# Six PSUM banks in one pool in place of two rings of three, in a kernel of two FFNs around a state-space layer

## What is computed

```python
def ffn(x):                                    # I = 2048 hidden
    h = silu(x @ w_gate) * (x @ w_up)
    return sparsify_2to4(h) @ w_down
def mamba(x):                                  # E = 1024, N = 16, after an RMS norm
    skip, u = xn @ W_skip.T, silu(causal_conv4(xn @ W_in.T) + conv_b)
    delta = softplus(u @ Wd1.T @ Wd2.T + bd2)
    h[l] = exp(delta[l] * A) * h[l-1] + delta[l] * u[l] * B[l]     # scan over 512 tokens, per (e, n)
    y = (sum_n h * C + u * W_D) * silu(skip)
    return y @ W_out.T
x = x + 0.5 * ffn(layernorm(x)); x = x + mamba(layernorm(x)); x = x + 0.5 * ffn(layernorm(x))
```

## Time and profile before

| | us |
|---|---|
| runs | 3585.91, 3588.35, 3592.87 |
| median | 3588.35 |
| profiled execution | 3583.97 |
| its span | 3582.0 |
| mean granted TensorE clock | 0.98 |

### The profile page before, as it was taken

One profiled execution on the slowest core, in us unless ns is written; L12 is line 12 of the kernel. 1 busy time (PEld: TensorE's weight loads), 2 busy tenths in 40 slices (PEclk: granted clock), 3 DMA queues, 4 the chain that ended last, 5 costly groups with the idle time before them and its releaser, 6 DMA issues. The chain is left out here.

```text
span 3582.0 us, 38967 instructions
## 1 busy us (share of the span) xinstructions
PE 3358.4 (94%) x11958; PEld 2126.1 (59%) x12020; DVE 3028.8 (85%) x3597; ACT 2001.7 (56%) x2760; POOL 2598.5 (73%) x1625
## 2 busy tenths in 40 slices
PE   8999999999999999999999999998979889988899
PEld 6775667556655665556655665555545555555567
DVE  5546998789999889989898899988998988999934
ACT  5546657557565665566555675555555566454422
POOL 1315876667877779868787789878888878989913
PEclk9999999999999999999999999999999989999999
DMA  9656566657656666466665675646646556545433
GB/s 361 218 188 194 171 211 214 212 177 223 211 182 215 199 222 211 158 211 214 185 210 179 203 229 177 217 147 210 222 125 211 169 179 220 189 146 190 138 124 115
DMA packets 243469, 696.44 MB, mean 194 GB/s; under 512 B 23536, under 2 KB 23792, under 8 KB 233584
## 3 DMA queue, kind: packets, MB, share of 16 engines
q1 hardware_dynamic: 173632, 559.72, 44.8%
q10 hardware_dynamic: 69632, 134.23, 14.2%
HBM read 619.94 MB, written 76.55 MB: 194 GB/s over the span
## 5 line engine op out<-in xcount | busy, mean ns | idle before, releaser
L1399 POOL TENSOR_TENSOR scan_in<-du,scan_rows 128x512 f32<-128x512 f32 x1024 | 1316.1, 1298 | 685.0 <-DVE decay L1273 595.1
L1273 DVE TENSOR_TENSOR_SCAN decay<-decay,scan_in 128x512 f32<-128x512 f32 x1024 | 1251.7, 1222 | 143.0 <-ACT decay L875 134.4
L875 ACT ACTIVATE decay<-delta,small 128x512 f32<-128x512 f32 x1024 | 699.1, 688 | 958.4 <-DVE scan_out L1283 952.1
L1412 POOL TENSOR_TENSOR y<-y,scan_out 128x1024 f32<-128x1024 f32 x512 | 1226.3, 2395 | 0.6 <-DVE scan_out L1283 0.6
L639 PE MATMUL main<-zhi,wunit 128*128 128x512 f32 x2048 | 910.0, 444 | 55.5 <-DVE cmp L1213 33.1
L641 PE MATMUL main<-zhi,wunit 128*128 128x512 f32 x2048 | 818.7, 400 | 0.0
L640 PE MATMUL main<-zlo,wunit 128*128 128x512 f32 x2048 | 817.4, 399 | 0.0
L731 PE MATMUL side<-h,wdown 128*128 128x512 f32 x1760 | 798.4, 597 | 18.0 <-ACT sq L1002 6.8
L1283 DVE TENSOR_TENSOR scan_out<-decay,scan_rows 128x512 f32<-128x512 f32 x1024 | 702.4, 686 | 27.6 <-POOL y L1412 2.1
L731 PEld LDWEIGHTS side<-h,wdown 128*128 128x128 f32 x1760 | 333.4, 191 | 384.5 <-issue 348.4
L862 ACT ACT_TABLE_LOAD x407 | 522.2, 1283 | 7.1
(11 more groups left out here) (109 smaller groups left out, 2862.5 us busy)
## 6 DMA issues: line engine op xcount, KB each, us to landing
wunit<-hl_dram SPq DMA_DIRECT2D x480, 512.0 KB, 4.4
scan_rows<-bc_dram ACTq DMA_DIRECT2D x256, 512.0 KB, 5.6
wdown<-down_w_dram SPq DMA_DIRECT2D x256, 256.0 KB, 3.2
wmam<-mam_dram SPq DMA_DIRECT2D x128, 512.0 KB, 4.0
hl_dram<-wunit SPq DMA_DIRECT2D x32, 512.0 KB, 5.3
skip_dram<-skb SPq DMA_DIRECT2D x64, 256.0 KB, 4.3
delta<-skip_dram SPq DMA_DIRECT2D x16, 1024.0 KB, 7.3
wmam<-wout_dram SPq DMA_DIRECT2D x32, 512.0 KB, 4.3
```

The costliest lines, as they stand in the source:

```text
L875: nc.scalar.activation(decay[u % BANKS][:], delta[:, e, :], ACT.Exp, scale=aneg[:, e * N + n:e * N + n + 1]).then_inc(sem["decay_ready"], 1)
L1273: nc.vector.tensor_tensor_scan(decay[u % BANKS][:], decay[u % BANKS][:], db[u % INPUTS][:], 0.0, ALU.mult, ALU.add).then_inc(sem["state_re ...
L1399: nc.gpsimd.tensor_tensor(db[u % INPUTS][:], du[:, e, :], rows[m % ROWS][:, 0, :], ALU.mult).then_inc(sem["input_ready"], 1)
L1412: nc.gpsimd.tensor_tensor(y[:, e:e + 2, :], y[:, e:e + 2, :], scan_out[:, k:k + 2, :], ALU.add).then_inc(sem["sum_ready"], 1)
```

## The change

The six banks become one pool, all named by number. A new step of the plan, `place_banks`, goes through all takes of a bank in TensorE's order. It gives each take a time at which it expects the bank's last reader to be done, in ticks: a gate 1.35 ticks after the pair's second gate, an up product 2.35 ticks after its own (1.55 for j = 0), a side job 1.1 to 1.9 ticks after its own. Each take gets the bank that by this is free first. The plan records the bank, its owner before, and for side jobs the running number of the read in that bank. TensorE then waits for the read of that owner (`wait_free`), be it a product or a side job. Readers take the bank from the plan. The order of the work on every queue stays as it was.

```diff
-MAINS = 3
-SIDES = 3
+POOL = 6
...
+    def place_banks(self):
+
+        read = {"win": 0.2, "down": 0.25, "out": 0.25, "mean": 0.3, "msum": 0.1, "vsum": 0.1, "in": 0.9, "var": 0.9}
+        takes = []
+        for tick, jobs in enumerate(self.jobs_at):
+            n = self.product_at[tick]
+            product = []
+            if n is not None:
+                s, j = divmod(pair_of(n), 4)
+                if not is_up(n):
+                    free = self.tick_of[4 * (n // 4) + 1] + 1.35
+                else:
+                    free = tick + (2.35 if j else 1.55)
+                product = [(("product", n), free)]
+            side = []
+            for key in jobs:
+                side.append((key, tick + 1 + read.get(key[0], 0.6)))
+                if key[0] == "var" and key[1] in self.alone:
+                    side.append((("awake", key[1]), tick))
+            early = n is not None and n % FFN == 0
+            order = side + product if early else product + side
+            takes += [(tick + k / len(order), key, free) for k, (key, free) in enumerate(order)]
+        free_at, owner, turns = [0.0] * POOL, [None] * POOL, [0] * POOL
+        self.bank_of, self.owner_before, self.turn_of = {}, {}, {}
+        for now, key, free in takes:
+            k = min(range(POOL), key=lambda k: (free_at[k], k))
+            self.bank_of[key], self.owner_before[key] = k, owner[k]
+            if key[0] != "awake":
+                owner[k] = key
+            if key[0] not in ("awake", "product"):
+                turns[k] += 1
+                self.turn_of[key] = turns[k]
+            free_at[k] = free
...
+            def wait_free(key):
+
+                owner = plan.owner_before[key]
+                if owner is None:
+                    return
+                if owner[0] != "product":
+                    wait_read(pe, owner)
+                    return
+                n = owner[1]
+                s, j = divmod(pair_of(n), 4)
+                if not is_up(n):
+                    pe.wait_ge(sem["gate_read"], 4 * s + j + 1)
+                elif j == 0:
+                    pe.wait_ge(sem["up_read"], 4 * s + 1)
+                else:
+                    pe.wait_ge(sem["compared"], 3 * s + j)
...
             def side_bank(key):
 
-                k = index[key]
-                if k >= SIDES:
-                    pe.wait_ge(sem[f"side_read_{k % SIDES}"], k // SIDES)
-                return side[k % SIDES]
+                wait_free(key)
+                return bank_of(key)
...
-                n = FFN * ORDER.index(plan.norms[i])
-                if n:
-                    pe.wait_ge(sem["up_read"], n // 2)
-                    pe.wait_ge(sem["compared"], 3 * (n // STEP))
+                wait_free(("awake", i))
```

More of the change, by code:

```diff
@@ L174, in __init__ @@
         self.place_weights()
+        self.place_banks()
     def place_projections(self):
@@ L340, in build @@
         halves = (slice(0, HE), slice(HE, KE))
-        main = [pb(f"main{k}") for k in range(MAINS)]
-        side = [pb(f"side{k}") for k in range(SIDES)]
+        banks = [pb(f"side{k}") for k in range(POOL)]
         decay = [pb(f"decay{k}") for k in range(BANKS)]
@@ L359, in build @@
             "skip_loaded_0", "skip_loaded_1", "bc_stored",
-            *(f"side_read_{k}" for k in range(SIDES)),
+            *(f"side_read_{k}" for k in range(POOL)),
             *(f"rows_loaded_{k}" for k in range(ROWS)),
@@ L380, in wait_read @@
         def wait_read(eng, key):
-            k = index[key]
-            eng.wait_ge(sem[f"side_read_{k % SIDES}"], k // SIDES + 1)
+            eng.wait_ge(sem[f"side_read_{plan.bank_of[key]}"], plan.turn_of[key])
         def conv_of(b, e):
@@ L420, in bank_of, with main @@
         def bank_of(key):
-            return side[index[key] % SIDES]
+            return banks[plan.bank_of[key]]
+        def main(n):
+            return banks[plan.bank_of["product", n]]
         def read_of(key):
-            return sem[f"side_read_{index[key] % SIDES}"]
+            return sem[f"side_read_{plan.bank_of[key]}"]
         def u_stores(b, e):
@@ L619, in _ @@
         def _(pe):
+            def wait_free(key):
[13 more added lines that the diff above has]
+                    pe.wait_ge(sem["compared"], 3 * s + j)
             def product(n):
                 i = n // FFN
[L623 to L630, removed]
+                wait_free(("product", n))
                 if i == 0:
@@ L638, in product @@
                         pe.wait_ge(sem["normed_ready"], KD * i + k + 1)
-                    nc.tensor.matmul(main[n % MAINS][:], hi[:, k, :], zhi[:, k, :], start=(k == 0), stop=False)
-                    nc.tensor.matmul(main[n % MAINS][:], hi[:, k, :], zlo[:, k, :], start=False, stop=False)
-                    mm = nc.tensor.matmul(main[n % MAINS][:], lo[:, k, :], zhi[:, k, :], start=False, stop=(k == KD - 1))
+                    nc.tensor.matmul(main(n)[:], hi[:, k, :], zhi[:, k, :], start=(k == 0), stop=False)
+                    nc.tensor.matmul(main(n)[:], hi[:, k, :], zlo[:, k, :], start=False, stop=False)
+                    mm = nc.tensor.matmul(main(n)[:], lo[:, k, :], zhi[:, k, :], start=False, stop=(k == KD - 1))
                 mm.then_inc(sem["product_ready"], 1)
             def side_bank(key):
-                k = index[key]
-                if k >= SIDES:
-                    pe.wait_ge(sem[f"side_read_{k % SIDES}"], k // SIDES)
-                return side[k % SIDES]
+                wait_free(key)
+                return bank_of(key)
             def quarters(key, x):
@@ L802, in keep_awake @@
             def keep_awake(i):
-                n = FFN * ORDER.index(plan.norms[i])
-                if n:
-                    pe.wait_ge(sem["up_read"], n // 2)
-                    pe.wait_ge(sem["compared"], 3 * (n // STEP))
+                wait_free(("awake", i))
                 for _ in range(AWAKE):
-                    nc.tensor.matmul(main[n % MAINS][:], pick[:], sq[:, KD - 1, :], start=True, stop=True)
+                    nc.tensor.matmul(banks[plan.bank_of["awake", i]][:], pick[:], sq[:, KD - 1, :], start=True, stop=True)
             def run_side(key):
@@ L899, in silu @@
                     wait_job(act, ("down", s - 2, KD - 1))
-                nc.scalar.activation(h[s % 2][:, j, :], main[gate_of(pair) % MAINS][:], ACT.Silu).then_inc(sem["gate_read"], 1)
+                nc.scalar.activation(h[s % 2][:, j, :], main(gate_of(pair))[:], ACT.Silu).then_inc(sem["gate_read"], 1)
             def magnitude(pair):
@@ L910, in magnitude @@
                 if j:
-                    nc.scalar.activation(main[(gate_of(pair) + 2) % MAINS][:], h[s % 2][:, j, :], ACT.Abs).then_inc(sem["magnitude_ready"], 1)
+                    nc.scalar.activation(main(gate_of(pair) + 2)[:], h[s % 2][:, j, :], ACT.Abs).then_inc(sem["magnitude_ready"], 1)
                 if j < 3:
@@ L1200, in multiply @@
                 dve.wait_ge(sem["gate_read"], pair + 1)
-                nc.vector.tensor_tensor(h[s % 2][:, j, :], main[(gate_of(pair) + 2) % MAINS][:], h[s % 2][:, j, :],
+                nc.vector.tensor_tensor(h[s % 2][:, j, :], main(gate_of(pair) + 2)[:], h[s % 2][:, j, :],
                                         ALU.mult).then_inc(sem["up_read"], 1)
@@ L1212, in compare @@
                     dve.wait_ge(sem["selected"], 4 * COUNTED.index(s - 1) + 4)
-                nc.vector.tensor_tensor(cmp[:, first:first + j, :], ab[:, 0:j, :], main[(gate_of(pair) + 2) % MAINS][:].unsqueeze(1).broadcast_to([P, j, L]),
+                nc.vector.tensor_tensor(cmp[:, first:first + j, :], ab[:, 0:j, :], main(gate_of(pair) + 2)[:].unsqueeze(1).broadcast_to([P, j, L]),
                                         ALU.is_ge).then_inc(sem["compared"], 1)
```

## The result

The changed kernel took 3548.99 us (median of four runs, 3544.95 to 3554.72) against 3588.17 (3585.91 to 3592.87): ratio 0.9892, 95% interval 0.988 to 0.9904, 39 us faster. The profiled execution is the slowest of its four, 3554.7 us with a span of 3552.8, so the two traces differ by 29 us only. A second profiled execution of the same kernel, in a later series, spans 3544.1.

The account below looks back on a forecast made before the run. TensorE early and VectorE late, both nearly full and tied by in-order queues, were taken to bound the kernel. Between gains of 33 and 85 us it took 50: 3588.35 - 50 = 3538, range 3500 to 3584.

Parts of the forecast that it names:

- Bank stalls are the two rings: TensorE in the scans: 76 stalls, 141 of 216 us idle, end on a ring bank's release; 67 (120 us) would go.
- Lower bound by single steps: Chain of waits through TensorE: 27 freed bank entries, smaller of entry and exit idle time each, summing to 32.6 us.
- new waits: TensorE takes that did not wait before but find their new bank still held: five takes, 1.7 us.
- Upper bound by stretch: Three scan stretches: TensorE's freed stalls plus clock loss, capped by VectorE's idle time traced to TensorE; 85 us together.
- the clock: TensorE's lower clock cost 20 us of work in 1400 to 2400 and 50 in 2400 to 3400, counted as recoverable.
- The choice between the bounds: Whole kernel: 50 us gain taken between 33 and 85, one bound being too small, the other needing more lead than banks hold.
- What is late next: After the change, the scan loop through ScalarE, then TensorE's waits for normed input and comparisons as data; no size given.
- The marks: Trace signs of being right or wrong: TensorE idle, late clock, VectorE's waits for TensorE, products behind compares, first stretch's length.
- Products stand behind side readers: 330 of 512 products take banks last read for side jobs; decides above 0.15 us mean wait, 3621 at 0.25; chance 0.08.
- VectorE binds: VectorE, 92% busy late in the scans, is the bound and nothing is won: 3581 to 3595; no gain either way 0.10.
- The lead feeds on itself: TensorE: fewer stalls, no clock drops, earlier exponentials shorten the scan loop too; 110 us, 3478; chance 0.10.
- The planner's due times are too rough: Bank choice by ticks, not microseconds, could be as poor as a ring, so no gain; no gain either way 0.10.

## Why the prediction was right, and where not

The forecast of 3538 (39 us measured against 50) stood on these steps.

**Bank stalls are the two rings.** Right. With sharing undone the time is that of before (1.0007), and 62 of the 67 takes that were to go free no longer wait. (The first bank stall of the scans is not the one at 351.90 in the earlier trace rows, which is the first of a product, but a projection's at 306.)

**Lower bound by single steps, 33 us.** It held, and was the better number. Idle time at the entry against idle time at the exit, along the chain of waits, is a reading that can be made on one trace, and the measured gain is 33 us from first to last product in the profiled execution, 38 in the second, and 39 by the medians. That it came out so close is in part luck: it counts only the last stall before each exit, and it has nothing in it for the 40 us of new waits.

**Upper bound by stretch, 18 + 37 + 30.** The sizes were two to three times too large: by the scans 7, 12 and 15 (9, 12 and 18 in the second execution). The 18 was all of TensorE's bank stalls early; 14 of them went and 7 became time. The 37 and 30 were all of VectorE's idle time that goes back to TensorE, and 24 and 9 us of it are still there. And in no stretch was the gain what TensorE gave back: that is 15, 13 and 21 us, and 9, 2 and 6 us came again as waits without TensorE. Two more terms were wrong, though the bound hardly hung on them. The first is the clock. I put 20 and 50 us down as something TensorE gets back (without them the bound is 81 in place of 85); time at 1.2 GHz went from 147 to 140 us, in the second execution to 126, worth 4 to 11 us of work at half speed. The clock falls around long stalls, as in the earlier trace rows, and there are 23 stalls of over 3 us now, 103 us together, and 20 with 95 us in the second execution (20 with 91 before): shorter stalls went, the long ones did not get fewer. The second is new waits: 1.7 us by the old times, 40 us in fact. The old times say when a bank was free for a TensorE that came late. One that comes earlier uses up the slack, so a count of takes with little slack (59 of 351 under 3 us) was the better warning than a sum of negative ones.

**The choice between the bounds.** This is the term that was mis-sized, 50 for 39. A third of the way up was too far, and what the sum lacked is a price for what is late next: the prediction named the loop through ScalarE and put it at nothing, and it took back 16 us. That TensorE gave back 49 us, close to the 50, is chance; the 50 was not worked out that way.

**What is late next.** Right in kind: data (75 to 107 us of TensorE's waits) and the loop through ScalarE (124 to 140 us of VectorE's idle time has no TensorE in it).

**The marks.** TensorE's idle time was to fall from 224 to 120 us. That was wrong by its own arithmetic: with unchanged work a gain of 50 leaves 174, and it is 194. The late clock at 0.98: wrong, 0.95 (0.96 in the second execution). VectorE's direct waits for TensorE under 40 us: wrong, 55 within the scans; only what went through ScalarE halved. Products behind their own ring's compare gone: right, none is left of 33 us. 300 to 1400 shorter by 10 to 18 us: right in kind, 7 to 9. Of the marks of being wrong, bank stalls under other names did come, but small: products behind h L1261, res_r and res_g are 21 us.

**The rivals.** "Products stand behind side readers" is real: 26 us of stalls over 328 such products (the prediction has 330), 0.08 us each, below the 0.15 from which it was to decide. And the run with fewer of them is slower, so it is not a cost of its own. "VectorE binds" is half right. A microsecond taken from VectorE is worth 0.36 to 0.48 us, one taken from TensorE's products in the rings 0.18 (88 of 477; 0.26 of the 345 by which its busy time fell), so VectorE is nearer to the bound; but a change on TensorE's side alone gave 39 us. The rule of the Trainium skill's page "Perfetto Trace Analysis", section "Identifying the Most-Contended Engine", names the right engine to work on first and is no argument that waits on the other are free. "The lead feeds on itself" did not come: VectorE's waits without TensorE grew, they did not shrink. "The planner's due times are too rough" was closer than I gave it credit for: with one common due time for side jobs three quarters of the gain are lost.

## What to carry to other kernels

Where two kinds of work leave an in-order engine in turns and their buffers are held for different times, one pool beats two rings of half the size (here five shared banks beat six split ones), but only with an order in which the buffers really come free; due times from a trace gained some 5 to 11 us more here. Cost such a change by the chain, entry against exit, and not by the sum of stalls that it frees: of 120 us of stalls that were to go some 105 went, and 39 us of time. When two traces are compared, cut them at the same work and not at the same microsecond. And an order made by a plan alone can make an engine wait for itself, so each change of the due times must be looked at for that.

## What the runs showed of the hardware

Executions of the changed kernel differed by TensorE's clock. Its first four had a mean granted clock of 0.979 and 0.980 with spans of 3550.6 and 3552.8 us, and twice 0.982 with 3543.2 and 3543.7. The two profiled ones span 3552.8 and 3544.1 us. Idle steps between weight loads are the same (239 and 241 us over 0.6 us each), and the time at 1.2 GHz is 140 and 126 us. At half speed 14 us more are some 7 us of work, most of the 9 us between them (an estimate from these numbers).

Less work on TensorE brought a lower clock: with 14% of its matmul time left out the granted mean fell from 0.980 to 0.936 in the rings, 0.948 in the pool. Busy time in the rings fell by 345 us and not by the 477 of the matmuls left out; the 301 us more at 1.2 GHz are up to 150 us of work at half speed, so they can account for the missing 132.
